# Attention over all tokens: one head group of every fourth block goes unsplit into a single fp32 value product

## The reference, cut to what matters

```
ca_q1  = einsum('btc,th->bch', ca, Wq_ca)       # 384 queries from 4 tokens
ca_hs1 = mha(ca_q1, residual, residual)         # softmax over all 2048 tokens, 8 heads
ca_q2  = ca_hs1[:, indices] @ Wq
ca_hs2 = mha(ca_q2, ca @ Wk_ca, ca @ Wv_ca)     # 4 keys
out    = (mha(x @ Wq, enc @ Wk, enc @ Wv) + ca_hs2) @ Wout + b_out + x
```

## Time and profile before

| | |
|---|---|
| median of 3 runs | 768.8 us (767.13 to 770.88) |
| the profiled execution | 769.75 us, of which the span from first to last instruction is 768.0 us |
| TensorE products (PE) | 725.4 us busy, 94% |
| TensorE weight loads (PEld) | 677.1 us, 88% |
| VectorE (DVE) | 564.1 us, 73% |
| ScalarE (ACT) | 375.9 us, 49% |
| GpSimd (POOL) | 171.4 us, 22% |
| mean granted TensorE clock | 0.982 |

### The profile page before, as it was taken

One profiled execution on the slowest core, in us unless ns is written; L12 is line 12 of the kernel. 1 busy time (PEld: TensorE's weight loads), 2 busy tenths in 40 slices (PEclk: granted clock), 3 DMA queues, 4 the chain that ended last, 5 costly groups with the idle time before them and its releaser, 6 DMA issues.

```text
span 768.0 us, 12603 instructions
## 1 busy us (share of the span) xinstructions
PE 725.4 (94%) x4693; PEld 677.1 (88%) x4693; DVE 564.1 (73%) x952; ACT 375.9 (49%) x942; POOL 171.4 (22%) x205
## 2 busy tenths in 40 slices
PE   7998999999899996968999999999999999799998
PEld 5978999999788886968899999999978887699997
DVE  3456888888899997436674888888889998656562
ACT  1634544454588962222333544455479994142330
POOL 8024951222100003502210521111110002211220
PEclk9999999999999999888999999999999999899999
DMA  8424353333400046697754334444230005578852
GB/s 275 144 94 124 69 125 90 90 90 90 145 30 1 0 76 157 137 218 183 151 139 101 65 90 109 102 98 94 90 129 2 0 1 128 131 159 188 177 124 74
DMA packets 227021, 82.37 MB, mean 107 GB/s; under 512 B 208324, under 2 KB 210372, under 8 KB 226960
## 3 DMA queue, kind: packets, MB, share of 16 engines
q1 hardware_dynamic: 226960, 81.56, 43.4%
HBM read 50.06 MB, written 31.39 MB: 106 GB/s over the span
## 4 chain that ended last, share of the span: by engine, by line
PE 80%; DVE 8%; SPq 3%; DMA 3%; issue 3%; ACT 2%; POOL 0%; DVEq 0%; POOLq 0%
PE PS L1230 30%; PE PS L1435 13%; PE PS L1418 6%; PE PS L1205 6%; PE PS L1305 6%; PE PS L1336 6%; PE PS L1327 5%; PE PS L1177 2%; SPq L432 2%; PE PS L1142 2%; DMA exT<-p_kept 2%; DVE pT_lo L1047 1%; SPq L479 1%; DVE res L1063 1%; PE PS L1188 1%
## 5 line engine op out<-in xcount | busy, mean ns | idle before, releaser
L1230 PE MATMUL PS<-mm_hi,xT_hi 128*128 128x280 f32 (+3 forms) x480 | 159.5, 332 | 0.0
L890 DVE TENSOR_REDUCE mpart<-PS 128x4 f32<-128x512 f32 x192 | 131.6, 687 | 36.9 <-PE PS L1205 36.7
L1230 PE MATMUL PS<-mm_hi,xT_lo 128*128 128x280 f32 (+3 forms) x480 | 157.4, 328 | 0.0
L1230 PE MATMUL PS<-mm_lo,xT_hi 128*128 128x280 f32 (+3 forms) x480 | 156.5, 326 | 0.0
L560 POOL TENSOR_TENSOR ex<-ex,rinv 128x992 f32<-128x992 f32 x30 | 55.4, 1845 | 201.5 <-DVE rinv L884 201.4
L666 ACT ACTIVATE ex<-PS,neg 128x124 f32<-128x124 f32 x256 | 89.9, 364 | 11.7 <-DVE gs L872 6.4
L1230 PEld LDWEIGHTS PS<-mm_hi,xT_hi 128*128 128x128 f32 x480 | 90.2, 188 | 0.7 <-issue 0.5
L1230 PEld LDWEIGHTS PS<-mm_lo,xT_hi 128*128 128x128 f32 x480 | 90.4, 188 | 0.3
L1230 PEld LDWEIGHTS PS<-mm_hi,xT_lo 128*128 128x128 f32 x480 | 90.3, 188 | 0.3
L754 ACT ACTIVATE oT_hi<-PS 128x256 fp32r<-128x256 f32 x80 | 29.5, 384 | 121.7 <-PE PS L1418 121.1
L608 POOL TENSOR_TENSOR xin<-xin,bias 128x640 f32<-128x640 f32 x32 | 49.8, 1562 | 160.6 <-DMA xin<-in_x 160.6
(11 more groups left out here) (154 smaller groups left out, 1355.9 us busy)
## 6 DMA issues: line engine op xcount, KB each, us to landing
ex_kept<-ex SPq DMA_DIRECT2D x32, 512.0 KB, 2.9
ex<-ex_kept SPq DMA_DIRECT2D x112, 128.0 KB, 3.1
xin<-in_x SPq DMA_DIRECT2D x128, 80.0 KB, 2.9
xin<-in_x SPq DMA_DIRECT2D x32, 320.0 KB, 3.5
out<-res SPq DMA_DIRECT2D x32, 320.0 KB, 2.3
raw_kept<-raw SPq DMA_DIRECT2D x5, 512.0 KB, 2.6
ex<-ex_kept SPq DMA_DIRECT2D x4, 512.0 KB, 3.8
mm_lo<-raw_kept SPq DMA_DIRECT2D x10, 186.0 KB, 4.4
```

The lines of the kernel that those rows point to most:

```text
L890: nc.vector.tensor_reduce(mpart[:, n // 2, :, 2 * (n % 2):2 * (n % 2) + 2, i].rearrange("p s k -> p k s"), PS[:, 6 + N % 2, :].rearrange(" ...
L1230: last = mul(PS[:, slot(T, k), p0:p0 + w], l[:, i % 2, j, :], rr[:, m0:m0 + w], start=(j == 0 and n == 0), stop=(n == 2), skip_group_check ...
```

## The change

For every fourth block (`p % 4 == 0`: 0, 4, ..., 28) the last head of the four is no longer split. The copy and the subtraction on VectorE work on the first three heads, 1152 columns. TensorE multiplies the last head's `e`, in fp32, with `ybuf` read as fp32, at the place of its high product, and its low product falls away. ScalarE's exponentials that reuse such a block's `e` buffer (blocks 3, 7, ...) also wait for that block's products.

```diff
--- before.py
+++ after.py
@@ -253,6 +253,10 @@
         def y_cols(h):
             return YC if h % 2 else 2 * YC
 
+        def split_heads(p):
+
+            return R - 1 if p % 4 == 0 else R
+
         def e_of(p):
             return e2nd[:, :] if p % E_BUFS == 2 else e01[:, p % E_BUFS, :]
 
@@ -707,6 +711,8 @@
                     act.wait_ge(sT_ps, N + 1)
                     if p >= E_BUFS:
                         act.wait_ge(elo_made, N - E_BUFS + 1)
+                        if split_heads(p - E_BUFS) < R:
+                            act.wait_ge(pv_done, N - E_BUFS + 1)
                     nc.scalar.activation(e_of(p), flat(sT_bank(p), 3), ACT.Exp, scale=SCALE).then_inc(e_made, 1)
                     if p == QUADS // 2 + 1:
                         take(0)
@@ -982,16 +988,18 @@
                         dve.wait_ge(e_made, N + 1)
                         if p >= HI_BUFS:
                             dve.wait_ge(pv_done, N - HI_BUFS + 1)
-                        nc.vector.tensor_copy(e_hi[:, p % HI_BUFS, :], e_of(p)).then_inc(ehd_made, 1)
+                        w = split_heads(p) * CAD
+                        nc.vector.tensor_copy(e_hi[:, p % HI_BUFS, 0:w], e_of(p)[:, 0:w]).then_inc(ehd_made, 1)
                         dve.wait_ge(ehd_made, b * QUADS // 2 + p // 2 + 1)
                     else:
                         dve.wait_ge(eha_made, b * QUADS // 2 + p // 2 + 1)
                     if p >= LO_BUFS:
                         dve.wait_ge(pv_done, N - LO_BUFS + 1)
-                    cols = (0, EW // 2, EW) if p + 1 == QUADS else (0, EW)
+                    w = split_heads(p) * CAD
+                    cols = (0, EW // 2, EW) if p + 1 == QUADS else (0, w)
                     for c0, c1 in zip(cols, cols[1:]):
                         nc.vector.tensor_tensor(e_lo[:, p % LO_BUFS, c0:c1], e_of(p)[:, c0:c1], e_hi[:, p % HI_BUFS, c0:c1].bitcast(F32), ALU.subtract)\
-                            .then_inc(elo_made if c1 == EW else ehalf_made, 1)
+                            .then_inc(elo_made if c1 == w else ehalf_made, 1)
                     if p == QUADS // 2:
                         take(0)
 
@@ -1324,13 +1332,17 @@
                             pe.wait_ge(nsa_made, SETS * b + 1)
                         if kt == 0 and s == 1 and r == 2:
                             pe.wait_ge(nsd_made, SETS * b + 1)
+                        if r >= split_heads(p):
+                            last = mul(PS[0:y_cols(r), 6 + r // 2, 0:CAD], y_of(kt, s * R + r).bitcast(F32), e_of(p)[:, r * CAD:(r + 1) * CAD],
+                                       start=False, stop=False, skip_group_check=True)
+                            continue
                         mul(PS[0:y_cols(r), 6 + r // 2, 0:CAD], y_of(kt, s * R + r), e_hi[:, p % HI_BUFS, r * CAD:(r + 1) * CAD],
                             start=(kt == 0 and r % 2 == 0), stop=False, skip_group_check=True)
                     if p + 1 == QUADS:
                         pe.wait_ge(ehalf_made, b + 1)
                     else:
                         pe.wait_ge(elo_made, N + 1)
-                    for r in range(R):
+                    for r in range(split_heads(p)):
                         if p + 1 == QUADS and r == R // 2:
                             pe.wait_ge(elo_made, N + 1)
                         last = mul(PS[0:y_cols(r), 6 + r // 2, 0:CAD], y_of(kt, s * R + r), e_lo[:, p % LO_BUFS, r * CAD:(r + 1) * CAD],
```

## The result

The changed kernel takes 774.45 us (median of 6 runs, 772.04 to 775.31) against 769.4 us of the kernel before in the same comparison (6 runs). The ratio is 1.0064, 95% interval [1.004, 1.0087]: slower by about 5 us. The prediction said 768.9, in a range of 767.2 to 772.3.

What follows compares the result with a forecast made beforehand. TensorE, at 9.16 us per four blocks, was taken to bound the changed attention stage. The terms (0.15 + 0.15 - 0.24) x 2 gave +0.1 us on the median of 768.8, so 768.9, range 767.2 to 772.3.

Steps and rivals of the forecast that it cites:

- The failed step: TensorE, attention stage: fp32 pair 0.656 us replaces two fp32r products, 0.350, weight loads hidden; +0.306 us per edited block.
- The sign that I had set for a wrong price: TensorE, attention stage: fp32 pair taking 0.8 us or more, or the edited group's step staying near 2.2, would refute the forecast.
- the slower one: Rival, TensorE: fp32 product drains the pipe on both sides or exposes weight loads (+0.25 us); up to 6 us; chance 0.09.
- a drained pipe at each passage: TensorE, before and after the fp32 pair: two drains make +0.79 us per edited block, +6 us in all.
- Two loops of equal length, relief in one: Attention stage: two loops through all engines, each 9.11 us per four blocks (one turn); VectorE's relief lies in only one.
- loop A: Loop through even blocks 4, 8, ..., 20, ...; waits in the stage's second half; forecast to fall from 9.11 to 8.33 us.
- loop B: Loop through even blocks 2, 6, 10, ...; waits in the stage's first half; forecast to keep its 9.11 us.
- TensorE sets the new turn and low products stop waiting: Attention stage: TensorE needs 9.16 us per four blocks, turn rises from 9.11 by 0.05, waits for low halves vanish.
- VectorE's saving: VectorE, copy and subtraction in edited blocks: 0.61 us less per turn, busy time down 9.7 us of 564.
- The start of the stage: Attention stage, block 0: TensorE's wait for block 2's low halves hides the added product; cost 0.
- Block 16: Change of key set: copy of finished sums 0.61 us earlier, block 19's scores 0.3 earlier; gain -0.24 us per batch.
- ScalarE's added wait costs nothing: ScalarE, before exponentials of blocks 3, 7, ...: wait for products of three blocks before is always met; cost 0.

## Why the prediction was wrong

- **The failed step** is "a load of 49 columns, 0.123 us, ends inside the product ahead, as it does today in a step of 0.175", and with it "Net 0.656 - 0.350 = +0.306 us per edited block". The rows quoted for the price had stationary operands of 80, 128 and 124 columns; the load row was that of an fp32r product. An fp32 product with 49 stationary columns costs 0.61 us net: 0.30 more. Seven edited blocks per batch lie in the flow (the eighth, block 0, is covered), 2 x 7 x 0.30 = 4.2 us, and the stages grew by 4.3. The width alone shows it: 65 columns bring the stages to 78.06 and 78.07 us, 0.04 above those of before together, and 98 columns the ratio to 1.0008. The sign that I had set for a wrong price, a pair of 0.8 us or more, did not come (0.77), because 0.18 of the 0.30 lie before and behind the pair.
- **The trace of before had the sign.** The set-up's line 1264 is an fp32 product with 8 stationary columns. Its loads, beside those of line 1257 (124 columns) ahead of it and of the fp32r products behind it:

```profile
44.04 0.94 PEld L1257 LDWEIGHTS PS<-wv_in,ctxT 128*124 128x124 f32 x4
...
50.81 0.10 PEld L1264 LDWEIGHTS PS<-wv_in,caT 128*8 128x8 f32 x2 [0.44 <-issue]
...
51.09 0.09 PEld L1264 LDWEIGHTS PS<-wv_in,caT 128*8 128x8 f32 x1 [0.18 <-issue]
...
53.51 0.09 PEld L1264 LDWEIGHTS PS<-wv_in,caT 128*8 128x8 f32 x1 [0.18 <-issue]
54.13 0.19 PEld L1230 LDWEIGHTS PS<-mm_hi,xT_hi 128*128 128x128 f32 x1 [0.54 <-issue]
```

```profile
50.81 3.40 PE L1264 MATMUL PS<-wv_in,caT 128*8 128x320 f32 x12
54.14 0.39 PE L1230 MATMUL PS<-mm_hi,xT_hi 128*128 128x280 f32 x1
54.37 0.29 PE L1230 MATMUL PS<-mm_hi,xT_lo 128*128 128x280 f32 x1
54.50 0.29 PE L1230 MATMUL PS<-mm_lo,xT_hi 128*128 128x280 f32 x1
```

The wide loads of line 1257 began at 44.04, 0.22 us before their product; the narrow ones begin with theirs, with 0.44 of idle put down to "issue", and so does the first load behind them, after 0.54. The first fp32r product there needs 0.23 us to the next, where the second needs 0.13. I took only the rate of such rows (0.28 us per record of 320 columns, narrow or wide) and missed that the price stands at their ends and grows out of the loads' starts. Inside the run of twelve narrow records there is no price: the loads' starts are 0.27 us apart (51.09 to 53.51 in nine steps), and the last load begins 0.27 us before the last record (at 53.78), one record ahead. So the price is paid where TensorE goes from another product into narrow fp32 ones and where it comes back, not for each narrow product; in the stage every narrow product stood alone between wide ones, which is why the two counts came out the same there.
- **The rival that came true** is the slower one, but by another road than the one written. It is not a drained pipe at each passage: the price of 0.79 is far above the 0.61, and passages with a wide load cost nothing. It is nearer to its second half, "or exposes its weight loads". I gave it 0.09 because of the transposes, whose stationary operand has 124 columns.
- **Two loops of equal length, relief in one:** right. The relief alone left the turn at 9.09 us and moved the late groups from loop A to loop B; taking it back left the turn at 9.43.
- **TensorE sets the new turn and low products stop waiting:** right; with the wide product the turn is 9.14 to 9.16 us as forecast.
- **VectorE's saving:** right, 9.9 us busy less for 9.7; the copy went to 0.76 us, the subtraction to 1.36.
- **The start of the stage:** right. From the key mask to the third block's low products it is 10.39 us before and after.
- **Block 16:** wrong in size. The step from the scores of block 17 to those of block 19 is 5.51 us (241.41 to 246.92 in the first batch) against 5.28 in the same batch of before (242.91 to 248.19); I expected 0.3 less than before. With 65 columns it is 5.19 (240.46 to 245.65), 0.09 less. VectorE's copy came 0.38 us earlier after block 17's scores (3.17 us behind their start, 3.55 before), not 0.61, since block 15's subtraction, ahead of it on VectorE, now waits for ScalarE's rounded exponentials (0.57 us of idle), and that wait I had left out.
- **ScalarE's added wait costs nothing:** right in this kernel, and only by TensorE's order; with the scores first it set the turn.

## What to carry to other kernels

When three engines run a loop within a few per cent of each other, list the loops by what they pass through and time each from rows; relief in one of two equal loops buys nothing, while issuing one group of scores ahead of the low products cut both loops and gave 0.6%. Price an operation by a row of the same type and the same stationary width that stands among the same neighbours, and look at when its loads begin, not only at its rate. And when a wait is free because of another engine's order, note which order, for the next reordering will make it due.

## What the runs showed of the hardware

- Behind a product of the same kind a weight load begins one record ahead of its own: 0.17 to 0.18 us ahead in the stream of fp32r products of 384 columns, whatever their width (98 or 49 columns; groups with both run at 0.70 us for four), and 0.27 us inside the narrow fp32 run of line 1264. An fp32 product with 65 stationary columns or more (65 and 98 behind fp32r products, 124 behind an fp32 one) has its loads as early as that too.
- Between a full fp32 product with 64 stationary columns or fewer (64, 49, 8) and a wide product, the load waits: going in, the narrow load begins only with its product, behind an fp32r product (64, 49) and behind a wide fp32 one alike (49 behind 98, 8 behind 124); coming out, the first load behind it does so (98 or 128 columns wide, idle 0.5 to 0.6 us). All products next to a narrow one had 98 columns or more; why the bound lies between 64 and 65 no run shows. That TensorE pulls weight loads ahead of running products is also what the Trainium skill says ("TensorE: Matmul & The Clock Gate", Architectural detail: the array is 16× 32×32, not 1× 128×128), without a bound by type or width; the runs with 64 and 65 columns show one.
- The price of one narrow fp32 product of 384 columns that stands alone among wide products is 0.30 us (0.10 before, 0.12 in it, 0.08 after), and twice that for two that stand apart (turns 9.43 and 10.02; 9.73 with one narrow and one wide). A run of them pays at its two ends only: line 1264's twelve records (8 columns) keep a step of 0.27 us inside; that this holds at 49 columns too is not shown. Two narrow products side by side in the stage were not tried. That it is the load's start that costs, and not something that delays both, is argued, not shown.
- An fp32 product between fp32r products with wide loads costs 0.65 us at 384 columns and no passage: 2 / 2.4 ns per column and a few ns per record, as in the set-up.
